# Early-fusion encoder layer: pair statistics from VectorE to ScalarE, counts behind the second pair's scores, expert weights split earlier

## The reference

```python
y = conv(x, W, stride 16) + b                   # 32 images, 14x14 patches, 192 channels
h = concat(y in Hilbert order (256 rows), txt (77 rows))        # (32, 333, 192)

q = layernorm(h)
k = grouped_pointwise(depthwise_conv9(q)) + pw_b                # 12 heads of 16
w = softmax(einsum(k * q, ak_w) + ak_b)                         # 9 weights a head and row
v = q @ pt_w.T + pt_b
h = h + sum over 9 taps of w[tap] * v[row + tap - 4]

xf = layernorm(h).reshape(-1, 192)                              # 10656 tokens
top2 of xf @ Wg; softmax over the two; positions in each expert by a running count, capped
for each expert: (a * silu(b)) @ W2 with a, b = xf @ W1, weighted, added to h at the tokens
```

## Time and profile before

| what | value |
|---|---|
| median of 3 runs | 1452.85 us (1452.49 to 1455.8) |
| the profiled execution | 1455.03 us, its span 1453.2 us |
| first block, about | 0 to 831 us of the span |
| mean granted clock | 0.907 |
| busy, share of the span | PE 83%, DVE 70%, POOL 48%, ACT 32% |

### The profile page before, as it was taken

How to read it: one execution, slowest core, us unless ns; L and a number is a source line. 1 busy time by engine, 2 the same in 40 slices (tenths; PEclk the granted TensorE clock), 3 DMA queues, 4 the chain that set the end, 5 groups by cost and what they waited for, 6 DMA issues and landing times. The chain is left out here.

```text
span 1453.2 us, 30800 instructions
## 1 busy us (share of the span) xinstructions
PE 1206.9 (83%) x8700; PEld 1012.7 (70%) x8701; DVE 1017.8 (70%) x2367; ACT 463.6 (32%) x1197; POOL 694.9 (48%) x530
## 2 busy tenths in 40 slices
PE   6987988998989898960642099999999999999995
PEld 6766777775767677640422078988898898898895
DVE  4117958999999999999576266666666666666663
ACT  2111222323223232311112254444444444444442
POOL 1000221666656666755647625544545454555454
PEclk9999999898999899885675599999999999999998
DMA  9995554565646363548611175544444444444442
GB/s 314 401 320 135 141 151 113 161 177 166 169 119 196 101 187 84 162 98 220 190 46 49 48 131 67 65 58 59 64 63 55 65 57 63 57 63 58 62 60 28
DMA packets 215171, 175.31 MB, mean 121 GB/s; under 512 B 121864, under 2 KB 198694, under 8 KB 215104
## 3 DMA queue, kind: packets, MB, share of 16 engines
q1 hardware_dynamic: 170128, 115.36, 32.7%
q0 software_dynamic: 34720, 34.38, 14.3%
q10 hardware_dynamic: 10256, 24.73, 4.6%
HBM read 69.24 MB, written 88.47 MB: 109 GB/s over the span
## 5 line engine op out<-in xcount | busy, mean ns | idle before, releaser
L1239 POOL DMA_INDIRECT out<-yb,meta x182 | 301.5, 1657 | 314.0 <-DMA out<-yb,meta 207.2
L129 POOL DMA_INDIRECT expert_inputs<-slot_rows,slots x176 | 236.5, 1344 | 85.5 <-issue 60.1
L1023 PE MATMUL bankK<-normedT,conv_w 128*128 128x333 f32 x864 | 277.2, 469 | 0.0
L1312 DVE TENSOR_TENSOR hidden<-silu,bankU 128x256 f32<-128x256 f32 x364 | 153.0, 421 | 136.6 <-PE bankU L1352 90.3
L1268 ACT ACTIVATE silu<-bankG 128x256 f32<-128x256 f32 x364 | 139.1, 383 | 301.7 <-PE bankG L1352 301.6
L1023 PEld LDWEIGHTS bankK<-normedT,conv_w 128*128 128x128 f32 x864 | 168.8, 201 | 77.7 <-issue 12.1
L1365 PE MATMUL bankY<-expert_weights,hidden_high 128*128 x728 | 179.2, 246 | 0.9 <-issue 0.2
L1366 PE MATMUL bankY<-expert_weights,hidden_high 128*128 x728 | 179.3, 246 | 0.0
L1367 PE MATMUL bankY<-expert_weights,hidden_low 128*128 x728 | 179.1, 246 | 0.0
L713 DVE TENSOR_TENSOR prod<-window_values,kb 128x960 f32<-128x960 f32 (+1 forms) x135 | 167.8, 1252 | 3.6
L731 DVE TENSOR_TENSOR hidden_group<-hidden_group,prod 128x960 f32<-128x960 f32 (+1 forms) x135 | 169.0, 1252 | 0.5
(11 more groups left out here) (162 smaller groups left out, 2294.9 us busy)
## 6 DMA issues: line engine op xcount, KB each, us to landing
patches<-in_x SPq DMA_DIRECT2D x16, 1536.0 KB, 8.9
expert_inputs<-prod ACTq DMA_DIRECT2D x6, 3430.0 KB, 23.3
token_rows<-rowbuf SPq DMA_DIRECT2D x32, 492.0 KB
window_values<-token_rows SPq DMA_DIRECT2D x32, 264.0 KB, 5.5
hidden_group<-token_rows SPq DMA_DIRECT2D x32, 264.0 KB, 7.1
window_values<-token_rows SPq DMA_DIRECT2D x32, 192.0 KB, 5.7
kb<-token_rows SPq DMA_DIRECT2D x32, 148.5 KB, 4.7
token_rows<-rowbuf SPq DMA_DIRECT2D x32, 148.0 KB
```

What stands on the lines that cost most here:

```text
L129: nc.gpsimd.indirect_dma_start(out=xslots[:, :], out_offset=bass.IndirectOffsetOnAxis(ap=idx[g % 2][:, k, r:r + 1], axis=0), in_=xrow[g % ...
L1023: mm = T_.matmul(bankK[(u + t) % 2][:, 0:L], conv_w[:, t // 2, k, :], qT[u][:, t, k:k + L], start=(k == 0), stop=(k == K - 1))
L1239: nc.gpsimd.indirect_dma_start(out=out[:, :], out_offset=bass.IndirectOffsetOnAxis(ap=meta[t % NMETA][:, c, 0:1], axis=0), in_=yb[v][:, c, ...
L1312: V.tensor_tensor(hf[j % 2][:, :], sg[j % 2][:, :], bankU[j][:, 0:TS], ALU.mult)\
```

## The change

- Statistics of a pair. `norm` on VectorE becomes `patches_out`, with the patch copies alone. ScalarE gets `moments(p)`: six Identity activations with scale -1/(192 sqrt(192)) whose accumulator gives a scaled negative mean, then six Square activations with that as bias and scale 1/sqrt(192) whose accumulator gives the variance. Their main outputs go into unused space of `qn`. The waits for text rows and for `ln_step` go along. GpSimd's `layer_norm` multiplies by sqrt(192) in place of -1 for pairs.
- ScalarE's order. `moments(p+1)` stands first in an iteration, then `normalise_slice(it-2, 0)` and `high_parts(it-2, 0)`, which stood at the end of the iteration before. `moments(p+2)` runs in fours behind the copies of `routing_out`.
- TensorE's order. `patch` comes before `transposes` in both halves; `counts_before(h)` comes after `scores(p+1)` and waits for its evacuation; `scores` waits for `pre_read` in both pairs.
- VectorE's order. `offsets` and `places` of a group move to the next iteration, behind `patches_out(p+1)`.
- Weights. `EARLY` is 3: experts 0 to 2 are split while the last group is normed and routed, 3 and 4 after `tile_list`; none at the start of the second block. A low part is done in 8 pieces. `prodL` moves to `w_all[:, 2]`.

```diff
-EARLY, MIDDLE = 2, 5
+EARLY, MIDDLE = 3, 5
...
         def split_high(act, e, raw):
-            wait(act, w_low, e - 1)
+            if e >= EARLY:
+                act.wait_ge(w_low, e - 1)
...
-        def split_low(dve, e, raw):
+        def split_low(dve, e, raw, pieces=1):
             dve.wait_ge(w_high, e + 1)
-            nc.vector.scalar_tensor_tensor(w_all[:, e, 1, :], raw, WSCALE, w_all[:, e, 0, :], ALU.mult, ALU.subtract)                .then_inc(w_low, 1)
+            for lo in range(0, WROW, WROW // pieces):
+                part = slice(lo, lo + WROW // pieces)
+                ins = nc.vector.scalar_tensor_tensor(w_all[:, e, 1, part], raw[:, part], WSCALE, w_all[:, e, 0, part],
+                                                     ALU.mult, ALU.subtract)
+            ins.then_inc(w_low, 1)
...
+                def moments(p):
+
+                    u = p % 2
+                    act.wait_ge(h_in_rows, 2 * p + 2)
+                    act.wait_ge(txt_loaded[u], 16 * (p // 2 + 1))
+                    wait(act, ln_step, NLN * p)
+                    wait(act, tq_ready, 3 * p - 3)
+                    settled(act)
...
+                    for n in range(6):
+                        ins = nc.scalar.activation(spare(n), rowb[u][:, n // 2, n % 2, D:2 * D], ACT.Identity,
+                                                   scale=-1 / (D * ROOT), accum_out=mean[:, n:n + 1])
...
+                    act.wait_ge(mean_done, p + 1)
+                    for n in range(6):
+                        ins = nc.scalar.activation(spare(n), rowb[u][:, n // 2, n % 2, D:2 * D], ACT.Square,
+                                                   bias=mean[:, n:n + 1], scale=1 / ROOT, accum_out=var[:, n:n + 1])
...
                         nc.scalar.copy(xTr[n % 2][:, :], bankT[n % 2][:, 0:384]).then_inc(tr_evac, 1)
+                        for _ in range(4 if beside else 0):
+                            next(beside, None)
...
+                    all_of(moments(p + 1))
+                    if it > 1:
+                        normalise_slice(it - 2, 0)
+                        high_parts(it - 2, 0)
                     normalise(p + 1)
...
+                    following = () if last(p + 1) else moments(p + 2)
                     if it > 1:
-                        routing_out(it - 2, 0, NQ)
+                        routing_out(it - 2, 0, NQ, following)
+                    else:
+                        all_of(following)
...
                 gate_exponential(NG - 2)
+                act.wait_ge(w_loaded[0], 64)
+                split_high(act, 0, raw0)
+                act.wait_ge(w_loaded[1], 64 * (E - 3))
+                split_high(act, 1, raw_at(3))
                 act.wait_ge(tap_summed, K)
...
                 ins.then_inc(sum_out, 1)
+                split_high(act, 2, raw_at(4))
...
                     attend(p, 0)
                     if it:
-                        norm(p + 1)
+                        patches_out(p + 1)
+                    if it > 2:
+                        offsets(h - 1)
+                        places(h - 1)
...
                         top_two(h)
-                    part(2)
-                    if it > 1:
-                        offsets(h)
-                        places(h)
-                    part(7 if it > 1 else 13)
+                    part(9 if it > 1 else 15)
...
                 slice_stats(g, 1)
+                for e in range(EARLY):
+                    split_low(dve, e, raw_at(e + 2) if e else raw0, pieces=8)
                 top_two(g)
                 offsets(g)
                 places(g)
                 tile_list()
-                split_low(dve, 0, raw0)
-                for e in range(1, EARLY):
-                    split_low(dve, e, raw_at(e + 2))
+                for e in range(EARLY, MIDDLE):
+                    split_low(dve, e, raw_at(e + 2), pieces=8)
...
-                    pe.wait_ge(kern_evac, 3 * min(2 * g + 5, NPAIR))
+                    pe.wait_ge(kern_evac, 3 * min(2 * g + 6, NPAIR))
...
-                    transposes(p + 1)
                     if p + 2 < NPAIR:
                         patch(p + 2)
+                    transposes(p + 1)
...
+                    if p + 3 < NPAIR:
+                        patch(p + 3)
                     if not last(p + 1):
                         transposes(p + 2)
-                    if p + 3 < NPAIR:
-                        patch(p + 3)
+                    for c in range(3):
+                        scores(p + 1, c)
                     if it > 1:
                         counts_before(h)
-                    for c in range(3):
-                        scores(p + 1, c)
```

More of the change, by code:

```diff
@@ L31 @@
 EPS = 1e-5
+ROOT = D ** 0.5
 NPAIR = B // 2
@@ L208, in build @@
             bankL = [bankK[0], bankK[1], bankH[0]]
-            prodL = [w_all[:, 1, u, 0:2 * SLICES[0][1] * D].bitcast(fp32) for u in range(2)]
+            prodL = [w_all[:, 2, u, 0:2 * SLICES[0][1] * D].bitcast(fp32) for u in range(2)]
             bankV = pb("bankV")
@@ L549, in high_parts, with routing_out @@
                     nc.scalar.copy(xrow16[g % 2][:, ss, 0:D], xn[:, ss, :]).then_inc(xh_ready, 1)
-                def routing_out(g, lo, hi):
+                def routing_out(g, lo, hi, beside=()):
                     for n in range(lo, hi):
@@ L567, in gate_exponential @@
                     nc.scalar.activation(ex[:, :], gap[:, :], ACT.Exp).then_inc(ex_ready, 1)
+                all_of(moments(0))
                 normalise(0)
@@ L596, in _ @@
                         high_parts(it - 2, 1)
-                    if it:
-                        normalise_slice(it - 1, 0)
-                        high_parts(it - 1, 0)
+                normalise_slice(NG - 2, 0)
+                high_parts(NG - 2, 0)
                 normalise_slice(NG - 2, 1)
@@ L637, in _, with patches_out @@
                 V.memset(zeros, 0.0).then_inc(zeroed, 1)
-                def norm(p):
+                def patches_out(p):
                     u = p % 2
@@ L647, in norm @@
                             .then_inc(h_in_rows, 1)
-                    dve.wait_ge(txt_loaded[u], 16 * (p // 2 + 1))
-                    dve.wait_ge(h_in_rows, 2 * p + 2)
-                    for c in (2, 0, 1):
-                        for m in range(2):
-                            ins = V.bn_stats(stats[:, 2 * c + m, :], rowb[u][:, c, m, D:2 * D])
-                    ins.then_inc(stats_done, 1)
-                    dve.wait_ge(stats_done, p + 1)
-                    wait(dve, ln_step, NLN * p)
-                    settled(dve)
-                    for n in range(6):
-                        ins = V.bn_aggr(mv[:, n, :], stats[:, n, :])
-                    ins.then_inc(aggr_done, 1)
                 def attend(p, t):
@@ L895, in _ @@
                 dve.wait_ge(first_loaded, 16 * NFIRST)
-                norm(0)
+                patches_out(0)
                 dve.wait_ge(const_loaded, NCONST)
@@ L922, in part @@
                         n -= 1
-                norm(1)
+                patches_out(1)
                 for it in range(NG):
@@ L944, in _ @@
                     if not last(p + 1):
-                        norm(p + 2)
+                        patches_out(p + 2)
                     part(6)
@@ L1043, in scores @@
                     wait(pe, kern_evac, 3 * p + c)
-                    if c == 0 and p > 3 and p % 2:
-                        pe.wait_ge(lg_read, p // 2 - 1)
-                        pe.wait_ge(pre_read, p // 2 - 1)
+                    if c == 0 and p > 3:
+                        if p % 2:
+                            pe.wait_ge(lg_read, p // 2 - 1)
+                        wait(pe, pre_read, p // 2 - 2)
                     T, n = CT[c], HA * K
@@ L1247, in _ @@
             def _(act):
-                for e in range(EARLY, MIDDLE):
-                    split_high(act, e, raw_of(e))
                 def body(i, tiles):
@@ L1277, in _ @@
                 V = nc.vector
-                for e in range(EARLY, MIDDLE):
-                    split_low(dve, e, raw_of(e))
                 def evac_y(i, t):
```

38 lines of the change are left out of this document (24 added, 14 removed).

## The result

The median of the changed kernel is 1430.98 us in four runs, of the kernel before 1452.67; the ratio is 0.9855, 95% interval 0.9824 to 0.9886. The four times are 1423.5, 1424.6, 1437.4 and 1443.2 us, with mean granted clocks of 0.915, 0.914, 0.903 and 0.900, where the kernel before has four times within 3.7 us. The median lies in the gap between the two short times and the two long ones; no run took it. The profiled execution is the first, 1423.54 us, span 1421.8: 31.5 us under the profiled one of before.

A forecast was written before the change was run, and what follows sets the result against it. VectorE was taken as the bound, TensorE close behind. Gains of 2+26+6+5 = 39 us from the median 1452.85 gave 1414, plus 1 for small waits: 1415 us, range 1399 to 1434.

The forecast's parts named there:

- Middle, 26 us: Middle of the attention stage: statistics off VectorE and fewer waits bring its period from 80.7 to 75.5, gaining 26 us.
- the loop is 73 us: Loop from moments through norm, router and TensorE to the next pair's convolution: 73 us, under VectorE's own period of 75.5.
- rival (1): A new wait in the router's loop, at 78, eats half the middle: 13 us there, 1427 in all; chance 0.2.
- 78 or more: Sign in the middle: a period of 78 us or more would show the prediction wrong.
- Moments, M = 6.6: ScalarE: a pair's 12 added activations take 6.6 us at 0.55 each; low end 5.5, high end 11.
- Rival (2): ScalarE's moments set the loop, a loss above 1.4 us an activation; at 1.6, 1476 us; chance 0.07.
- Rival (3): ScalarE's table changes, 1.28 us twice a pair, make the loop 75.6 and the time 1417; chance 0.07.
- Start and first groups, 2 gained: Up to 218 us: later first norm against patches covering TensorE's waits; 2 us gained, ends -6 and +9.
- Last group, 6: Last group: loads about 10 us earlier, scatters 5, Exp 5 to 6; 6 us gained, ends 0 and 8.5.
- Splits, 5: Weight splits moved into pauses and cut in pieces, freeing the last scatters: net 5 us gained, ends 1 and 8.
- 1.3 lost: Within the splits: moved ones touch slice norm, low_parts and a scatter or two, losing 1.3 us.
- Granted clock of 0.95 or more: Sign in the middle: TensorE's granted clock at 0.95 or more would show the prediction right.

The follow-up runs named there:

- experiment 6: The changed kernel again, unedited, on chip 4: 1443.9, 1426.0, 1440.7 and 1439.9 us, ratio 0.9873 to the kernel before.
- experiment 3: The changed kernel with the pair norm's statistics back on VectorE for all pairs, on chip 10: 1468.58 us.
- experiment 8: The changed kernel with statistics of pairs 0 and 1 on VectorE, pieces stopped for GpSimd's low part, and two exponential reorderings, chip 4: 1411.1 to 1429.0 us, ratio 0.9751.
- experiment 2: The changed kernel with the old weight splits back, each whole, on chip 10: 1482.29 us.
- experiment 1: The changed kernel again, unedited, on chip 10: 1475.64 us, 1.0099 of the kernel before.
- experiment 4: The changed kernel with VectorE stopping its pieces after the tenth of 24 until GpSimd's first low part of the last group, chip 10: 1470.85 us.
- experiment 9: The changed kernel with the counts back ahead of the second pair's scores, on chip 10: 1470.90 us.
- experiment 10: The changed kernel with the pair norm's statistics back on VectorE, run a second time on chip 10: 1470.24 us.
- the last version: The four edits of experiment 8 on the changed kernel, plus the second score block in bank V: 1447.11 us on chip 10, 1410.49 us on chip 11.

## Why the prediction was right, and where it was not

Its range, 1399 to 1434, holds the median of the four runs, and "faster" came true. Its 1415 us stands 16 us below. That the median lies in the range is in part luck: it needed two short executions of four. The long ones, 1437 to 1444 us, are outside it, and so is the median of experiment 6, 1440.3. On chip 10 its sign would have been wrong.

- **Middle, 26 us.** In the short execution 27.3 us, period 75.2 for a forecast of 75.5, and by the reason given: work taken off VectorE, which then waits for no convolution. TensorE waited for normalised rows once in the five iterations, 1.5 us, so the later norm was covered. The step that failed is the sentence before it, "the loop is 73 us": it was summed with TensorE's convolutions at 5.2, and only this loop was held against VectorE. The leg from one pair's last convolution to the next pair's first was not. There the change leaves no slack, and five of the eight executions of the changed kernel outside chip 10 are long; the one of them with a trace has a period of 78.5. That is rival (1)'s number, 78, but not its mechanism: the router's hand-overs did not bind; TensorE waited 6.0 us for xTr over the five iterations, never over 1.4, and 7.4 in the short execution, never over 1.8. (The rows sum to 72.4 for the loop, not 73; nothing hangs on it.) The sign "78 or more" was named and was the one that came.
- **Moments, M = 6.6.** 4.95 us, 5.7 among the router's copies, at the low end of 5.5: the row it came from, 0.457, is of activations with scale and bias both from memory; the Square here takes its bias from there, 0.44, the Identity neither, 0.35. The second instruction for the accumulator came, as the high end had it, but costs almost nothing. Rival (2) needed 1.4 us an activation. Rival (3) falls: one table load, so the Trainium skill's price of a change ("ScalarE: Activation LUTs", What ACT_TABLE_LOAD costs) was never paid.
- **Start and first groups, 2 gained.** 3 lost in the short execution, 6.5 in the long one; inside -6 to +9 or just past it. The first half was mostly right (TensorE stands 3.6 us longer and loses 1.8 to the clock, where the prediction had 6 and 3); of the 15.6 us of waits that patch should cover 11.9 stayed, and the waits for VectorE's values bank grew from 2.9 to 6.0. Experiments 3 and 8 price it: some 10 us with all statistics on VectorE, 4 to 7 with those of pairs 0 and 1.
- **Last group, 6.** 4.2. The weight loads came only some 5 us earlier against VectorE, and GpSimd stood as long, 8.10. The sign "near 7 us" for the exponential was missed, with 9.48. Experiment 8 shows that no more was to be had from it: TensorE's router is late next.
- **Splits, 5.** 2.6 in the traces, 3.9 and a median of 6.6 in experiment 2. The gain was as said: of the last 22 scatters the first takes 1.26 us, all others 0.97 to 1.01. The term "1.3 lost" was mis-sized: "beside a whole split" had been read of scatters, and GpSimd's tensor operation is held by the back-to-back pieces to 5.48 us, 4.6 lost. That is also the rule of the Trainium skill ("SBUF — State Buffer", Who interferes with whom) that the prediction had named, and had turned the wrong way: cutting an instruction does not end the hold if the next piece follows at once.
- **Granted clock of 0.95 or more.** 0.95 and 0.98 in the short execution, 0.91 in the long one. This was the sign to have priced. The counts' pause, 0.57 us, came as said.

How the 27 us of the middle divide between moments, patches and counts is measured for one iteration alone, the one without the stall in experiments 1 to 4, 9 and 10: the moments' 4 to 5 us are all of its gain. The kernel with the statistics back ran on chip 10 alone, so for the other four iterations the division is not measured.

## What to carry to other kernels

When a change takes work off the bounding engine, add up the next engine's own chain between each two hand-overs, once at either clock level, not only its busy time: where the first engine's work fell between the two sums, this kernel got two times. Look for stops to take out of that chain (here by a second PSUM bank) before taking more work off the first engine. And run on more than one chip: a gain of 1.5% here was a loss of 1% there.

## What the runs showed of the hardware that was not expected

- An activation of 192 columns with an accumulator costs ScalarE 0.35 (Identity) or 0.44 us (Square), though it is written as two instructions (0.351 or 0.443, and 0.187 inside it).
- VectorE's 0.44 us pieces with two SBUF inputs, back to back, held a GpSimd tensor operation of 0.91 us for 5.48 us. One wait of VectorE between pieces brought it back to 0.91.
- One chip of the three of the experiments showed TensorE standing, by its late semaphores some 4 to 7 us, in each iteration with 22 scatters or more and not in the one with seven, with events missing from the trace there; across chips the kernel before took 8 us more on it, the changed one 35 or more, the last version 37.
- The same kernel (experiment 8) ran with periods of 75.5 and 75.9 us and then of 78.3 to 78.5, within one execution.
